# Householder tridiagonalisation: the new column from one packed product, a part formed beside the inner product, and another order of two waits on ScalarE

## The reference

```python
h = jnp.maximum(_layernorm(x, axis=-1), 0.0)          # x: 128 x 128 nodes x 128 features, float32
x = x + _L0_gnn_ref(h, adj, ...)
h = jnp.maximum(_layernorm(x, axis=-1), 0.0)
x = x + _L1_gnn_ref(h, adj, ...)                       # two graph convolutions, then four small LSTMs

def _L0_gnn_ref(features, A, W1, b1, W2, b2):
    deg = jnp.sum(A, axis=0) + jnp.sum(A, axis=1) - jnp.diagonal(A)
    d_inv_sqrt = jnp.where(deg > 0, jax.lax.rsqrt(deg), 0.0)
    L = jnp.diag(deg) - A
    L_norm = d_inv_sqrt[:, None] * L * d_inv_sqrt[None, :]
    _, U = jnp.linalg.eigh(L_norm)                     # 128 x 128
    agg = jnp.einsum('mn,bnd->bmd', U.T, features)
    h = jax.nn.relu(agg @ W1 + b1)
    out = h @ W2 + b2
    return jnp.einsum('nm,bmd->bnd', U, out)
```

## Time and profile before

| | |
|---|---|
| median of three runs | 1539.92 us (1539.84 to 1540.45) |
| the profiled execution | 1543.1 us, span 1541.4 us |
| busy: TensorE, VectorE, ScalarE, GpSimd | 78%, 73%, 52%, 32% of the span |
| L931, the inner product, between 20 and 395 us | 125 times, 283 ns each |
| L597, the row of the product, two passes a step | 441 ns a pass |

### The profile page before, as it was taken

One profiled execution on the slowest core, in us unless ns is written; L12 is line 12 of the kernel. 1 busy time (PEld: TensorE's weight loads), 2 busy tenths in 40 slices (PEclk: granted clock), 3 DMA queues, 4 the chain that ended last, 5 costly groups with the idle time before them and its releaser, 6 DMA issues.

```text
span 1541.4 us, 26140 instructions
## 1 busy us (share of the span) xinstructions
PE 1202.5 (78%) x7121; PEld 1074.2 (70%) x7121; DVE 1130.8 (73%) x6077; ACT 795.0 (52%) x2572; POOL 495.6 (32%) x1426
## 2 busy tenths in 40 slices
PE   5667777777626500079899999999999999999998
PEld 4556666666515400068689889898998989989897
DVE  8999999999999999968756545555555554645545
ACT  1222222222319800012378688786877868778676
POOL 0288888888888888800000000000000000000000
PEclk9999999999959955569999999999999999999999
DMA  9300000000000000002100000000000000000000
GB/s 268 74 1 0 1 1 1 1 1 1 1 1 1 1 0 1 0 28 86 52 1 1 28 0 14 14 0 27 0 14 14 0 27 0 19 8 0 28 1 28
DMA packets 43625, 28.76 MB, mean 19 GB/s; under 512 B 1520, under 2 KB 39440, under 8 KB 43536
## 3 DMA queue, kind: packets, MB, share of 16 engines
q1 hardware_dynamic: 43536, 27.81, 6.6%
HBM read 19.42 MB, written 8.39 MB: 18 GB/s over the span
## 4 chain that ended last, share of the span: by engine, by line
PE 56%; DVE 38%; issue 3%; ACT 3%; ACTq 0%; DVEq 0%
PE bank L788 13%; PE bank L778 9%; PE bank L783 7%; PE bank L791 7%; PE bank L597 6%; DVE PV L1188 5%; DVE RC L1182 4%; DVE PV L1118 2%; DVE wB L931 2%; PE bank L710 2%; PE bank L718 2%; PE bank L752 2%; PE bank L760 2%; PE bank L746 2%; DVE sc L941 2%
## 5 line engine op out<-in xcount | busy, mean ns | idle before, releaser
L788 PE MATMUL bank<-spare,wT 128*128 128x256 f32 (+2 forms) x1408 | 311.3, 321 | 0.0
L528 ACT ACTIVATE PV<-bank,bias 128x256 f32<-128x256 f32 (+2 forms) x704 | 304.1, 435 | 0.0
L528 ACT ACTIVATE BIG<-bank,bias 128x128 f32<-128x128 f32 (+2 forms) x544 | 227.6, 418 | 118.2 <-PE bank L791 101.9
L788 PEld LDWEIGHTS bank<-spare,wT 128*128 128x128 f32 x1408 | 234.8, 191 | 13.2
L778 PE MATMUL bank<-spare,wT 128*128 128x128 f32 (+2 forms) x1088 | 228.1, 320 | 4.4 <-DVE spare L1424 2.9
L1410 DVE TENSOR_TENSOR BIG<-BIG,PV 128x128 f32<-128x128 f32 (+2 forms) x192 | 63.0, 328 | 209.8 <-ACT BIG L528 209.7
L778 PEld LDWEIGHTS bank<-spare,wT 128*128 128x128 f32 x1088 | 168.7, 190 | 22.9 <-DVE spare L1424 9.5
L791 PE MATMUL bank<-spare,wT 128*128 128x128 f32 (+2 forms) x768 | 169.7, 303 | 0.0
L423 ACT ACTIVATE sc<-bank 128x1 f32<-128x1 f32 x127 | 21.7, 171 | 262.9 <-PE bank L592 262.9
L592 PE MATMUL bank<-ident 128*128 128x2 f32 x254 | 74.3, 362 | 93.2 <-DVE ident L947 92.1
L783 PE MATMUL bank<-spare,wT 128*128 128x128 f32 (+2 forms) x768 | 141.5, 307 | 3.6 <-DVE spare L1422 1.4
(11 more groups left out here) (393 smaller groups left out, 2769.4 us busy)
## 6 DMA issues: line engine op xcount, KB each, us to landing
spare<-in_x SPq DMA_DIRECT2D x32, 256.0 KB, 3.8
out<-X SPq DMA_DIRECT2D x32, 256.0 KB, 2.4
spare<-in_L_gnn_Wih SPq DMA_DIRECT2D x4, 256.0 KB, 5.1
spare<-in_L_gnn_Whh SPq DMA_DIRECT2D x4, 256.0 KB, 5.1
W<-in_L_gnn_W SPq DMA_DIRECT2D x2, 64.0 KB, 2.5
Wg<-in_L_gnn_Wg SPq DMA_DIRECT2D x2, 64.0 KB, 2.3
adj<-in_adj SPq DMA_DIRECT2D x1, 64.0 KB, 1.9
X<-in_x SPq DMA_DIRECT2D x4, 0.5 KB, 17.2
```

Source lines behind the costliest of these rows:

```text
L528: last = nc.scalar.activation(gate_out[q][i][:, 0:T], gate(i, q, T), ACT.Tanh if q == GATE_G else ACT.Sigmoid, bias=bias[:, at:at + 1])
L788: last = nc.tensor.matmul(gate(i, q, T), wT[:, 0, p - 1, q * D:(q + 1) * D], xt, start=True, stop=(j == 0))
```

## The change

The new column is written as K times one packed vector, less a part R. With H = h * masked x * u_t (HG), V = h * mask * u_t (HV) and HUM = h * masked x:

    x = HG * K - (p * HV + (HUM * row_t - ACOL))

- UC grows from 3 to 5 columns a step; its first column is now the mask itself, not its negative. A new two-element multiplication makes `UC[:, k, 3:5]` = `UC[:, k, 0:2]` * u_t, behind h. It waits for u_t.
- The packed product with h takes `UC[:, k, 1:5]`, four elements (HUM, HU, HV, HG). It waits for the new multiplication, for u and, new at this place, for ScalarE's row.
- PT = HUM * row_t - ACOL is new. It waits for TensorE's row and for the packed product, and stands ahead of the inner product.
- L935 and L937 are gone. R takes the place of L941 and waits for p and for PT. The last instruction is HG * K3 - R.
- On ScalarE the two waits ahead of the root change places: `s_ready` first, `e_ready` second.

```diff
-        UC = sb("UC", [N, N, 3])
+        UC = sb("UC", [N, N, 5])
...
                 t = k + 1
+                act.wait_ge(s_ready, k + 1)
                 if k >= 2:
                     act.wait_ge(e_ready, k - 1)
-                act.wait_ge(s_ready, k + 1)
...
-            op(V.tensor_scalar(UC[:, 0:N - 1, 0], below[:, 1:N], -1.0, None, ALU.mult))
+            op(V.tensor_copy(UC[:, 0:N - 1, 0], below[:, 1:N]))
...
                 n_h = step(V.reciprocal(h_k, S(DEN)))
-                dve.wait_ge(hv, n_h)
+                dve.wait_ge(hv, n_ut)
+                n_mu = step(V.tensor_scalar(UC[:, k, 3:5], UC[:, k, 0:2], u_t, None, ALU.mult))
+                dve.wait_ge(hv, n_mu)
                 dve.wait_ge(u_ready, k + 1)
-                n_nh = step(V.tensor_tensor(S(HB, 3), UC[:, k, :], h_k.to_broadcast([N, 3]), ALU.mult))
-
-                dve.wait_ge(pb_ready, k + 1)
                 if t + 1 < N:
                     dve.wait_ge(row_ready, k + 1)
+                n_nh = step(V.tensor_tensor(S(HUM, 4), UC[:, k, 1:5], h_k.to_broadcast([N, 4]), ALU.mult))
+
+                dve.wait_ge(pb_ready, k + 1)
+                dve.wait_ge(hv, n_nh)
+                n_pt = step(V.scalar_tensor_tensor(out=S(PT), in0=B[1][:, nxt], scalar=S(HUM), in1=S(ACOL),
+                                                   op0=ALU.mult, op1=ALU.subtract))
                 n_k = step(V.tensor_tensor_reduce(out=wB[:, live(k)], in0=banks[1][:, live(k)], in1=uk[:, live(k)],
                                                   scale=h_k, scalar=0.0, op0=ALU.mult, op1=ALU.add,
                                                   accum_out=S(K3)))
-                dve.wait_ge(hv, n_nh)
-                n_v = step(V.tensor_tensor(S(V1), S(HB), u_t, ALU.mult))
-                dve.wait_ge(hv, n_k)
-                n_z = step(V.scalar_tensor_tensor(out=S(Z), in0=u_t, scalar=S(K3), in1=B[1][:, nxt],
-                                                  op0=ALU.mult, op1=ALU.subtract))
                 dve.wait_ge(p_ready, k + 1)
-                dve.wait_ge(hv, n_v)
-                n_t2 = step(V.scalar_tensor_tensor(out=S(T2), in0=banks[2][:, 0:1], scalar=S(V1), in1=S(ACOL),
-                                                   op0=ALU.mult, op1=ALU.add))
+                dve.wait_ge(hv, n_pt)
+                n_r = step(V.scalar_tensor_tensor(out=S(R), in0=banks[2][:, 0:1], scalar=S(HV), in1=S(PT),
+                                                  op0=ALU.mult, op1=ALU.add))
                 n_nhp = step(V.scalar_tensor_tensor(out=S(NHP), in0=banks[2][:, 0:1], scalar=-1.0, in1=h_k,
                                             op0=ALU.mult, op1=ALU.mult))
-                dve.wait_ge(hv, n_t2)
-
-                V.scalar_tensor_tensor(out=x_c, in0=S(HUM), scalar=S(Z), in1=S(T2),
-                                       op0=ALU.mult, op1=ALU.add).then_inc(x_ready, 1)
+                dve.wait_ge(hv, n_r)
+
+                V.scalar_tensor_tensor(out=x_c, in0=S(HG), scalar=S(K3), in1=S(R),
+                                       op0=ALU.mult, op1=ALU.subtract).then_inc(x_ready, 1)
```

More of the change, by code:

```diff
@@ L189, in build @@
         STEPS = N - 1
-        ST, DEN, SGE1, SGE, K3, NHP, V1, T2, Z, ACOL = range(10, 20)
-        HB, HUM, HU = range(20, 23)
+        ST, DEN, SGE1, SGE, K3, NHP, PT, R, ACOL = range(10, 19)
+        HUM, HU, HV, HG = range(20, 24)
         def two_sigma(k):
```

## The result

The changed kernel takes 1552.32 us (median of four runs, 1551.26 to 1553.23) against 1539.88 on the same occasion: ratio 1.0077, 95% interval 1.0062 to 1.0093, so it is slower by 12.4 us, 9.5 to 14.3. The forecast was 1552.0, slower.

What follows compares the result with a forecast made beforehand. Each step is one closed chain, mostly VectorE's, repeated about 126 times. Thirds of +0.04, +0.11 and +0.145 us a step, less 0.2 for early products, plus 0.2 for clearing, gave 12 on 1539.92: 1552, range 1540 to 1558.

Steps and rivals of the forecast that it cites:

- (a): Ahead of L911: ScalarE's root (L423) sets its start in the late step, VectorE's own queue in the early step.
- (b): Between L921 and L947: L931 waits for TensorE's product, leaving 0.13 us empty early and hardly any late.
- The three prices: VectorE: dependent start 0.03 to 0.04 us; second wait 0.105; one element without scalar about 0.15, two with scalar 0.229.
- the bounds at 0.15 and 0.25: Limits for the new multiplication's length: 0.15 us if its scalar were free, 0.25 at most; 0.229 was taken.
- The chain to PT: Starts behind L921: multiplication +0.245 us, packed product +0.509, PT +0.777, with PT waiting for VectorE alone, not TensorE.
- Behind K: From the inner product K to the new column x: chain shorter than before, x at +1.416, +1.366 and +1.355 us.
- The sum over the steps: 42 x (0.04 + 0.11 + 0.145) = 12.4 us slower, about 0.2 taken off for longer early products.
- the samples: Three single steps of the tridiagonalisation read in the timeline, early, middle and late, each standing for 42 steps.
- the late +0.205 a step: Late-step slowdown in us: x at 1.355 against 1.15 before; +0.145 once the root's 0.06 is counted.
- The root's wait: L423 on ScalarE starts 0.06 us earlier; this moves L911 only in the late third, 42 x 0.06 = 2.5 us.
- the clearing: Clearing UC, 640 instead of 384 elements a partition, ahead of VectorE's first real instruction: 0.2 us more, once.
- The rival of the hidden vector: PT starts 0.04 us after TensorE's product; 0.13 a step gained, 16.4, plus the root's 2.5: 1521; chance 9%.

Runs made afterwards that it cites:

- a1_root_only: Kernel before with only ScalarE's two waits ahead of the root exchanged; 1537.75 us against 1540.91, ratio 0.9980.
- b2_fused: Changed kernel with HV and HG made by one instruction from u_t and h, not waiting for the packed product; 1529.15 us against 1541.72 for the kernel before.
- a3_pt_order: Changed kernel with the two waits ahead of PT exchanged, so PT carries the packed product's; 1543.63 us against 1540.91 for the kernel before.
- a4: Changed kernel with a second scalar from memory (ones) in the new two-element multiplication; 1561.12 us against 1540.91 for the kernel before.
- a2_root_undone: Changed kernel with ScalarE's two waits ahead of the root back in the old order; 1554.56 us against 1540.91 for the kernel before.
- b0_changed: Changed kernel once more, unaltered, for comparison on another chip; 1552.54 us against 1541.72 for the kernel before, ratio 1.0072.
- b3_fused_order: b2_fused with PT's two waits in the other order from step 75 on; 1528.55 us against 1541.72 for the kernel before.
- b4_third_wait: Changed kernel with a third wait, on u, ahead of PT; 1550.25 us against 1541.72 for the kernel before.

## Why the prediction was right, and what it sized wrongly

- What bounds a step, places (a) and (b): right. a1_root_only moved the late steps most and the first ones hardly; in the early step PT cannot start before TensorE's product, in b2_fused as in L931 before.
- The three prices: right to 0.01. Dependent start 0.035, second wait 0.105, the multiplication 0.228 against the 0.229 of its twin L1330, the bounds at 0.15 and 0.25 not needed. a3 and a4 each changed one of them alone, and the steps followed.
- The chain to PT: predicted +0.245, +0.509, +0.777, read +0.25, +0.51, +0.78.
- Behind K: predicted x at +1.416, +1.366, +1.355; read +1.40, +1.35, +1.35. R takes 0.21 where its start is set by the inner product, not L941's 0.22, and the step from R to x is 0.25 instead of 0.255.
- The sum over the steps: predicted 12.2, read 10.0. By thirds (L947 number 1, 43, 85 and 127) the steps grew by 1.2, 3.7 and 5.2 us where the samples gave 1.7, 4.6 and 6.1. a2_root_undone has VectorE's half alone: 1.3, 4.4 and 7.4, where the samples gave 1.7, 4.6 and 8.6. So the mis-sized term is the late +0.205 a step, which measures 0.175. The larger part of it is the base: the sample read x at +1.17 before, and that is the median of the last 42 steps; the prediction took 0.02 off because L935 was long in it.
- The root's wait: 2.5 predicted, 3.2 measured by a1 (3.6 in the steps), 2.7 to 3.2 within the changed kernel. It also gives 0.6 in the middle third, where 13 of 42 steps are behind ScalarE and the sample was not.
- So the prediction's 12 and the measured 12.4 agree better than their parts do, and part of that agreement is luck: the steps and the clearing explain 10.2, and the rest is within what separates executions of one kernel. The kernel before was 1539.88, 1540.91 and 1541.72 on three occasions, and the changed one 10.8 us over it in b0's comparison.
- The rival of the hidden vector failed for its mechanism: in the changed kernel PT never starts right behind TensorE's product. Its price of 0.13 a step holds only for the first third (b2_fused against a1_root_only: 0.13, 0.08 and -0.01 a step), so with the link taken out the time is 1529 and not that rival's 1521.
- The rule of the Trainium skill, page "VectorE: DVE Perf Modes", section "The DRAIN you can't avoid", that a semaphore costs nothing extra between chained operations, does not hold here. The page measured it on eight copies that took 13.88 us together; most operations here take 0.15 to 0.23 us. The changed kernel, a3_pt_order and b2_fused have equally many VectorE operations a step, and their steps take 387.4, 379.3 and 365.4 us. For these short operations the number of links and the wait that is carried decide.

## What to carry to other kernels

On a chain of one-element instructions count links, not instructions: a link costs the predecessor's whole length and 0.035 us, an instruction beside it 0.07 to 0.135 us. Before an idle gap is filled, compare its length (0.13 us here, and shrinking) with the chain that has to run before it, and build what goes in from values that are ready early. Where an instruction has several waits, write the one that comes last first, so that the instruction carries it: that alone took 3.6 us off the steps of the kernel before and 8.1 off those of the changed one. It gains only as much as the two waits lie apart: in b3_fused_order the other one came 0.04 us earlier and took over.

## What the hardware showed unexpectedly

A wait more made the steps shorter: with three waits ahead of PT, two share one sequencer entry and PT starts 0.09 instead of 0.105 behind what it waits for (b4_third_wait, 0.9 to 1.4 us in 126 steps). Why the shared entry is left sooner was not found out.

The span behind the steps differs between executions of equal work. The windows of the stretch between the eigenvectors and the first layers (us, busy times of TensorE, its weight loads, VectorE, ScalarE and GpSimd, PEclk the granted TensorE clock, DMA share, GB/s), for the kernel before, the changed one and the changed one again (b0_changed):

```profile
674.90:682.70 7.80, 7.80 (x43) 7.80 (x44) 0.31 (x2) 2.75 (x4) 0.00 (x0) 0.60 0.00 0
```

```profile
685.20:691.50 6.30, 6.30 (x43) 6.30 (x44) 0.28 (x1) 2.75 (x4) 0.00 (x0) 0.75 0.00 0
```

```profile
685.30:692.90 7.60, 7.60 (x43) 7.60 (x44) 0.28 (x1) 2.75 (x4) 0.00 (x0) 0.62 0.00 0
```

The same 43 products took 7.80, 6.30 and 7.60 us at a mean granted clock of 0.60, 0.75 and 0.62 of 2.4 GHz: TensorE came into the stretch at 1.2 GHz, after little work (busy for 12 of the 137 us ahead of it in the kernel before), and the clock rose to 2.4 GHz at 681.1, 688.3 and 691.1. Between the two executions of the changed kernel that makes 1.3 us in this stretch, as much as what lies behind the steps differs by (1147.3 and 1148.7 us). All ten profiles go together in this way: the rise comes 285.6 to 289.0 us behind the last L947, what lies behind the steps takes 1146.9 to 1149.3 us, and where the one is longest or shortest so is the other. The four runs of the changed kernel lie at 1551.3, 1551.4, 1553.2 and 1553.2, about that far apart; that this is their cause was not tested, nor what sets the moment of the rise. For a change of 10 us in a stage ahead of it, the steps in the profile are the surer measure.
